# A graph-attention layer on one core: 39 output projections moved into the edge loop

## The reference

```
h     = relu(layernorm(x))
q,k,v = h wq + bq, h wk + bk, h wv + bv
score = q[dst].k[src] / 16 + edge_weight we + be        one number per edge
attn  = softmax of the scores of the edges with one destination
out   = sum over those edges of attn * v[src]
y     = layernorm(h + out + h ws + bs) g1 + b1
z     = layernorm(y + gelu(y w1 + b_ff1) w2 + b_ff2) g2 + b2
result = x + z
```

## Time and profile before

| | us |
|---|---|
| median of 3 runs (3053.38 to 3068.75) | 3056.34 |
| the profiled execution | 3050.0 |
| its span, first to last instruction | 3048.2 |
| PE busy, share of the span | 2431.4 (80%) |
| DVE | 1749.3 (57%) |
| POOL | 1632.3 (54%) |
| ACT | 1152.5 (38%) |

### The profile page before, as it was taken

One profiled execution on the slowest core, in us unless ns is written; L12 is line 12 of the kernel. 1 busy time (PEld: TensorE's weight loads), 2 busy tenths in 40 slices (PEclk: granted clock), 3 DMA queues, 4 the chain that ended last, 5 costly groups with the idle time before them and its releaser, 6 DMA issues. The chain is left out here.

```text
span 3048.2 us, 66637 instructions
## 1 busy us (share of the span) xinstructions
PE 2431.4 (80%) x15042; PEld 2006.5 (66%) x15043; DVE 1749.3 (57%) x7385; ACT 1152.5 (38%) x2601; POOL 1632.3 (54%) x1828
## 2 busy tenths in 40 slices
PE   6877778777777777787878778878877887879998
PEld 5666566666566666666666656666666666758897
DVE  7655555555455555555555555555555565557777
ACT  6433333333333333333333333333333333335666
POOL 5455555555555555555555555545555555451254
PEclk8988889888889889898888899999999898989999
DMA  7333333333333333333333333333333333233122
GB/s 237 97 106 108 108 108 102 108 96 113 95 104 104 104 97 106 102 105 104 97 100 97 102 93 102 108 90 99 102 101 106 92 101 105 86 98 103 52 82 66
DMA packets 148147, 311.29 MB, mean 102 GB/s; under 512 B 33566, under 2 KB 84625, under 8 KB 148104
## 3 DMA queue, kind: packets, MB, share of 16 engines
q0 software_dynamic: 75264, 205.62, 23.2%
q1 hardware_dynamic: 54718, 90.19, 9.1%
q10 hardware_dynamic: 18122, 14.96, 1.6%
HBM read 290.21 MB, written 20.43 MB: 102 GB/s over the span
## 5 line engine op out<-in xcount | busy, mean ns | idle before, releaser
L508 POOL DMA_INDIRECT work<-h_rows,idx x1536 | 1454.9, 947 | 1159.6 <-SPq L390 766.0
L1085 PE MATMUL bank<-work 128*128 x3528 | 1003.1, 410 | 125.7 <-ACT work L649 100.8
L1050 PE MATMUL bank<-q,onehot 128*128 x5316 | 746.0, 292 | 119.2 <-DVE norms L859 112.8
L1085 PEld LDWEIGHTS bank<-work 128*128 128x128 f32 x3528 | 652.9, 206 | 211.2 <-issue 143.8
L1050 PEld LDWEIGHTS bank<-q,onehot 128*128 128x128 bf16 x5316 | 548.6, 104 | 247.3 <-issue 99.5
L649 ACT COPY work<-bank 128x512 f32<-128x512 f32 x440 | 258.4, 587 | 1059.0 <-remote 609.9
L859 DVE SCALAR_TENSOR_TENSOR norms<-bank,work 128x257 bf16<-128x257 f32 x1326 | 503.8, 424 | 206.8 <-remote 167.4
L1056 PE MATMUL bank<-ident,mean 128*128 128x128 f32 x1764 | 296.7, 294 | 310.1 <-DVE mean L916 267.7
L1056 PEld LDWEIGHTS bank<-ident,mean 128*128 128x128 f32 x1764 | 211.0, 145 | 397.3 <-DVE mean L916 241.1
L859 DVE SCALAR_TENSOR_TENSOR work<-bank,work 128x257 bf16<-128x257 f32 x442 | 188.1, 425 | 445.1 <-remote 321.9
L916 DVE CUSTOM_DVE_ANT_0 work<-bank,work,mean 128x512 f32<-128x512 f32 x440 | 328.6, 747 | 115.7 <-issue 57.9
(11 more groups left out here) (200 smaller groups left out, 1726.9 us busy)
## 6 DMA issues: line engine op xcount, KB each, us to landing
dst_words<-dst_short SPq DMA_DIRECT2D x99, 512.0 KB
work<-h_rows,idx POOLq DMA_INDIRECT x1568
bias<-h_rows ACTq DMA_DIRECT2D x56, 128.0 KB
r_rows<-bias ACTq DMA_DIRECT2D x55, 128.0 KB
work<-r_rows SPq DMA_DIRECT2D x49, 128.0 KB, 2.6
h_rows<-acc SPq DMA_DIRECT2D x12, 512.0 KB, 6.8
work<-in_x SPq DMA_DIRECT2D x12, 512.0 KB, 3.9
out<-work SPq DMA_DIRECT2D x48, 128.0 KB, 1.8
```

Of the source, the lines that this page charges most:

```text
L508: pool.indirect_dma_start(rows[:, u, j, 0:D], None, h_rows, bass.IndirectOffsetOnAxis(idx[:, half, u * J + j:u * J + j + 1], 0)).then_inc( ...
L1050: last = nc.tensor.matmul(banks[j][:, 0:D1], onehot[:, k, j, :], q3[:, bass.ds(b, 1), c, 0:D1], start=(c == 0), stop=(c == 2))
L1085: last = nc.tensor.matmul(banks[6 + k][:, 0:D1], probs[k][:, j, :], rows[:, bass.ds(slot, 1), j, :], start=(j == 2), stop=(j == 1))
```

## The change

For blocks 0 to 38 (`LOOPED`) the trip computes all of y but its bias: `h (ws + 1) + bs + (sums / weight) wv`. The result is written over the block's sums in `acc`; nothing is stored in HBM. The other 10 blocks (`TAIL`) get both projections in the output stage.

- A block may be taken when its last step is done. ACT keeps the number of the next block in registers, and in step 2 of each trip reads the table of steps and moves on to the next block if that is ready, or else to a spare block (`NB`, zeros with a huge weight), whose result is thrown away (`choose_next`). The number of trips is the larger of what the steps need and 39 plus the largest lead, a lead being the trip in which a block is finished less its number.
- DVE floors and inverts all weights in step 0 of each trip. ACT weighs one block's sums in step 1.
- PE turns h at the end of steps 0 and 1, the weighed sums at the end of 2 and 3, and projects at the end of 5 and 6, each half with a bias matmul, two by ws and two by wv. wv is loaded once, before the loop, into rows that hold biases otherwise.
- ACT copies the turned halves in steps 1 to 4 before it copies the probabilities, and the halves of y in steps 6 and 7 behind the probabilities. L872 waits for these copies in the same steps.
- The store of r in the trip and the loads of r are gone. The output stage loads h of the 10 tail blocks, and PE turns both h and sums there. DVE adds weight * bv in place (one instruction where there were two) and takes the statistics; 30 looped blocks come among the tail's, 9 inside the feed-forward stage. The norm's factors are made for blocks 0 to 19, and later for the rest.

```diff
+    LOOPED = B * 4 // 5
+    TAIL = B - LOOPED
+    MOST_TRIPS = TRIPS + LOOPED + 1
+    ASIDE = 6
...
-        acc = sb("acc", [P, NB, D1])
+        acc = sb("acc", [P, NB + 1, D1])
...
-                def copy_r(turn, n):
-
-                    if n == 1:
-                        act.wait_ge(r_stored, turn * 16 + 16)
-                    act.wait_ge(r_ready, turn * 2 + (2 - n))
-                    nc.scalar.copy(r_out[:, n * P:(n + 1) * P], banks[6 + n][:, R_AT:R_AT + P]).then_inc(r_copied, 1)
-
-                def store_r(turn):
-
-                    act.wait_ge(r_copied, turn * 2 + 4)
-                    act.dma_start(r_rows[bass.ds(turn % B * P, P), :], r_out).then_inc(r_stored, 16)
+                def choose_next(r, i):
+
+                    at = table_place(act, place_in_table, i)
+                    act.load([last_seen], steps_tab[0:1, bass.ds(at + (U - 2), 1)])
+                    done = block_of(act, act.snap(last_seen, min_val=0, max_val=(B + 1) * CHUNKS) + r * ROUND)
+                    act.reg_alu(last_seen, act.to_reg(done), LOOPED, ALU.min)
+                    act.reg_add(block_next, next_block, 1)
+                    act.reg_alu(last_seen, last_seen, block_next, ALU.min)
+                    act.reg_sub(block_next, last_seen, block_next)
+                    act.reg_alu(block_next, block_next, 63, ALU.bitwise_and)
+                    act.reg_alu(block_next, block_next, next_block, ALU.bitwise_or)
+                    act.reg_alu(block_next, block_next, NB, ALU.min)
+                    act.reg_mov(next_block, last_seen)
+
+                def weigh_e(b):
+
+                    nc.scalar.activation(u_e, acc[:, bass.ds(b, 1), 0:D].rearrange("p a d -> p (a d)"), ACT.Copy, scale=inv_e[:, bass.ds(b, 1)]).then_inc(weighed, 1)
+
+                def copy_aside(turn, n, to, bank):
+
+                    act.wait_ge(side_ready, turn * ASIDE + n)
+                    nc.scalar.copy(to, banks[bank][:, R_AT:R_AT + P]).then_inc(side_copied, 1)
+
+                def copy_y(b, n):
+
+                    nc.scalar.copy(acc[:, bass.ds(b, 1), n * P:(n + 1) * P].rearrange("p a d -> p (a d)"), banks[6 + n][:, R_AT:R_AT + P]).then_inc(side_copied, 1)
...
-                        if steps == U and u in (2, 3):
-                            copy_hTe(act.snap(act.to_reg(r * NW + i), min_val=0, max_val=B * NW), u - 2)
-                        if steps == U and u in (5, 6):
-                            copy_r(act.snap(act.to_reg(r * NW + i), min_val=0, max_val=B * NW), 6 - u)
+                        if steps == U and u in (1, 2):
+                            copy_aside(turn, u, hT_e[:, (u - 1) * P:u * P], 6 + u % 2)
+                        if steps == U and u in (3, 4):
+                            copy_aside(turn, u, uT_e[:, (u - 3) * P:(u - 2) * P], 6 + u % 2)
+                        if steps == U and u == 1:
+                            act.wait_ge(inv_done, turn + 1)
+                        if steps == U and u in (6, 7):
+                            act.wait_ge(side_ready, turn * ASIDE + (u - 1))
                         act.wait_ge(turned, s + 1)
                         nc.scalar.copy(probs[k][:].rearrange("p j n -> p (j n)"), banks[5][:]).then_inc(probs_done, 1)
+                        if steps == U and u == 1:
+                            weigh_e(here)
+                        if steps == U and u in (6, 7):
+                            copy_y(here, u % 2)
+                        if steps == U and u == 2:
+                            choose_next(r, i)
+                            load_h_of_next()
...
+                        if steps == U and u == 0:
+                            turn = dve.snap(dve.to_reg(r * NW + i), min_val=0, max_val=B * NW)
+                            floor_at, aside = dve.to_reg(turn + 1), dve.snap(dve.to_reg(turn * ASIDE), min_val=0, max_val=B * NW * ASIDE)
+                            dve.wait_ge(added, step)
+                            nc.vector.tensor_scalar(floor_e, acc[:, 0:NB + 1, D], 1e-12, None, ALU.max).then_inc(floor_done, 1)
                         edge_scores(step_at(regs[u + 2]), r, prepared, k, meanwhile)
                         here = block_at(u)
+                        if steps == U and u == 0:
+                            dve.wait_ge(floor_done, floor_at)
+                            nc.vector.reciprocal(inv_e, floor_e).then_inc(inv_done, 1)
...
-                        if steps == U and u in (2, 3):
-                            dve.wait_ge(hTe_copied, dve.to_reg((r * NW + i) * 2 + (u - 1)))
-                        if steps == U and u in (5, 6):
-                            dve.wait_ge(r_copied, dve.to_reg((r * NW + i) * 2 + (u - 2)))
+                        if steps == U and u in (1, 2, 3, 4, 6, 7):
+                            dve.wait_ge(side_copied, dve.to_reg(aside + (ASIDE + u - u // 6)))
                         add_sums(s, u + 2, dve.snap(held[u], min_val=0, max_val=B) if u < 2 else blocks[u - 2])
...
+                def project_both(aside, n):
+
+                    y = banks[6 + n][:, R_AT:R_AT + P]
+                    if n == 0:
+                        pe.wait_ge(late_in, 5 * 16)
+                        pe.wait_ge(side_copied, aside + (ASIDE + 4))
+                    nc.tensor.matmul(y, onesb_rows, s_bias3[:, n * P:(n + 1) * P], start=True, stop=False)
                     for c in range(DC):
+                        nc.tensor.matmul(y, hT_e[:, c * P:(c + 1) * P], ws_sb[:, c, n * P:(n + 1) * P], start=False, stop=False)
+                    for c in range(DC):
+                        last = nc.tensor.matmul(y, uT_e[:, c * P:(c + 1) * P], wv_e[:, c, n * P:(n + 1) * P], start=False, stop=(c == DC - 1))
+                    last.then_inc(side_ready, 1)
...
-                        if steps == U and u in (1, 2):
-                            turn_h(pe.snap(pe.to_reg(r * NW + i), min_val=0, max_val=B * NW), u - 1)
-                        if steps == U and u in (4, 5):
-                            project_h(pe.snap(pe.to_reg(r * NW + i), min_val=0, max_val=B * NW), 5 - u)
+                        if steps == U and u in (0, 1):
+                            turn_h(turn, aside, u)
+                        if steps == U and u in (2, 3):
+                            turn_u(turn, aside, u - 2)
+                        if steps == U and u in (5, 6):
+                            project_both(aside, u - 5)
...
+                def add_bias(b):
+
+                    y = acc[:, b, 0:D]
+                    if b >= LOOPED:
+                        dve.wait_ge(o_ready, b - LOOPED + 1)
+                        y = banks[2 + tail_bank(b - LOOPED)][:, 0:D]
+                    nc.vector.scalar_tensor_tensor(out=acc[:, b, 0:D], in0=row_of["bv"], scalar=weight_sum[:, b:b + 1], in1=y, op0=ALU.mult, op1=ALU.add).then_inc(y_done, 1)
...
-                for b in range(3):
-                    add_bv(b)
-                add_output(0)
-                for b in range(1, B):
+                for n in range(AFTER_TAIL):
+                    b = y_order[n]
                     if b == B - 1:
                         copy_yT(0)
-                    add_output(b)
-                    measure(b - 1, y_done, FIRST_NORMS)
+                    next_y(n)
...
+                    for n in range(AFTER_TAIL + 2 * b, min(AFTER_TAIL + 2 * b + 2, B)):
+                        next_y(n)
```

More of the change, by code:

```diff
@@ L91, in gnn_layer @@
         wv_sb = sb("wv_sb", [P, DC, D])
[L92 to L95, removed]
+        bias = sb("bias", [P, 6, D])
+        row_of = {n: bias[:, k, :] for n, k in (("bs", 0), ("g1", 0), ("b2", 1), ("b_ff2", 2), ("bv", 3), ("g2", 4))}
+        h_in, hT_e, u_e = (bias[:, k, :] for k in range(3))
+        uT_e = u_e
+        wv_e = bias[:, 4:6, :]
         bff1_col = sb("bff1_col", [P, FC])
@@ L140, in gnn_layer @@
         ws_sb = wv_sb[:]
+        floor_e, inv_e = (ones[:, k * (NB + 1):(k + 1) * (NB + 1)] for k in range(2))
         wqk = halves(DC * D1)
@@ L1030, in _ @@
                         nc.tensor.matmul(chunk_of_step, shift_chunks, in_block, start=True, stop=True)
+                        nc.tensor.matmul(lead_row, lead_f, ident[:, 0:LOOPED], start=True, stop=True)
                         pe.wait_ge(falls_done, 2)
@@ L1114, in _ @@
                 keep_busy(banks[5], 14)
+                place_in_table = pe.alloc_register("place_in_table")
                 def trip(r, i, steps):
-                    pe.load(regs[0:steps + 3], steps_tab[0:1, bass.ds(i * U, steps + 3)])
+                    pe.load(regs[0:steps + 3], steps_tab[0:1, bass.ds(table_place(pe, place_in_table, i), steps + 3)])
+                    turn = pe.snap(pe.to_reg(r * NW + i), min_val=0, max_val=B * NW)
+                    aside = pe.snap(pe.to_reg(turn * ASIDE), min_val=0, max_val=B * NW * ASIDE)
                     first = pe.snap(pe.to_reg(r * TP + i * U), min_val=0, max_val=B * TP)
@@ L1171, in gnn_layer @@
         fT = slots(2, F)
+        both_T = fT
+        X_AT = used[0]
```

(39 more changed lines are left out.)

219 lines of the change are left out of this document (126 added, 93 removed).

## The result

The changed kernel takes 3206.05 us (median of 6 runs, 3188.02 to 3220.54) against 3058.07 us (6 runs, 3045.65 to 3068.84): 1.0477 times the time, 95% interval 1.0432 to 1.0522 (ratios here are of the runs' means). It is slower by 148 us; the forecast was 3138 in a range of 3030 to 3215.

The account below looks back on a forecast made before the run. It took a chain of hand-overs between engines, 6.07 us a step, to bound the edge stage. Edge +108 and output -26 gave +82 on the profiled 3050.0; 6 more for the median made 3138 us, range 3030 to 3215.

Parts of the forecast that it names:

- The loop that no longer stays loaded: Rival, edge stage: the longer trip fetches its code every trip, 114 us more, 3252 us; chance 0.04.
- Output stage, -26: Output stage: fewer DVE instructions per block bring the first feed-forward matmul 30 us after the first weighing, gaining 26 us.
- Copies of y, +44: Edge stage, steps 6 and 7: DVE's addition waits for ACT's copies behind the probabilities; 0.8 us a trip, 44 us.
- PE, +33: Edge stage: added turns and projection passes, 1.32 us a trip at full clock, partly hidden; 0.6 counted, 33 us.
- the 0.2 that was to show a larger share of PE: Sign: free steps near the edge stage's end growing over 0.2 us would mean PE's share was taken too small.
- ACT's code, +22: Edge stage, steps 1 and 2: weighing, table read, block choice and load of h cost 0.4 us a trip, 22 us.
- DVE, +14: Edge stage, step 0: floor and reciprocal of the weights cost 0.25 us a trip, 14 us.
- The -5 us for the store: Edge stage: dropping ACT's store of r at the trip's end saves 0.1 us a trip, 5 us.
- the rival that the holds swallow the added work: Rival, edge stage: gathers' end releases steps, so added work lies in existing waits; 3036 us, faster; chance 0.15.

Follow-up runs that it names:

- e2: The kernel before with 20 one-column memsets at VectorE's start, its loop otherwise untouched: 3119.75 us, ratio 1.0232 to the kernel before.
- e5: The changed kernel with 96 one-column memsets at VectorE's start, moving its loop: 3129.49 us, ratio 1.0126 to the kernel before.
- e12: e9 with ScalarE's weighing and block choice ahead of the probabilities' copy, 33 blocks in place of 40 before the feed-forward stage: 3094.09 us, ratio 0.9990.
- e9: Changed kernel, VectorE's loop moved on by 88; y copies ahead of the probabilities' copy, their wait on a one-column copy behind the mask's: 3106.45 us, ratio 1.0039.
- e6: e5 with the copies of y ahead of the probabilities' copy, waiting for the projection before the mask's copy: 3113.39 us, ratio 1.0062 to the kernel before.
- e8: e5 without the two wv passes in each of a trip's two projections: ratio 1.0115 to the kernel before.
- e10: e9 without ScalarE's block choice, PE's wv passes and VectorE's floor and reciprocal: 3085.14 us, ratio 0.9994 to the kernel before.
- e7: e5 without ScalarE's choice of the next block in step 2, always taking the spare one: ratio 1.0095 to the kernel before.
- e11: The kernel before with 96 memsets at VectorE's start: 3098.72 us, ratio 1.0018 to the kernel before.
- e1: The changed kernel with 40 one-column memsets at VectorE's start, nothing in the loop altered: 3206.1 us, ratio 1.0523 to the kernel before.
- e3: The changed kernel with ScalarE's copies of y ahead of the probabilities' copy, waiting for the projection before the mask's copy: 3165.55 us, ratio 1.0386.
- e4: The changed kernel with both e1's 40 memsets and e3's order of the copies of y: 3138.70 us, ratio 1.0292 to the kernel before.

## Why the prediction was right in direction and wrong in its sum

**The loop that no longer stays loaded** is the step that failed. The forecast read the earlier trace rows as a reason to leave it at 0.04: no trip fetches now. But 20 and 23 packets say only that the loop of today stays, not how near it is to its limit, and e2 shows that 20 instructions were enough. Its price, 114 us in the forecast, was measured at about 107 by e5, and at 71 to 122 by other pairs of runs. The loss is smaller than VectorE's 157 us of later first instructions (172 against 15 in e5), as steps 0 and 1 behind the stall shorten. That the time still fell inside the range is luck: a cost forecast at nothing was made up for in part by other terms that were forecast too high. The Trainium skill (Runtime: NRT & Kernel Launch, section Instruction fetch mechanics) has the rule that bears on it: a taken branch to a target outside the current two-page window waits for a fetch of that page. The five 8 KB packets in every trip agree with it in kind. It was cited, and then priced by a row that couldn't speak against it.

**Without it** the forecast was +82 us; e5's 1.0126 is +39 (20 to 57), so the other terms were forecast too high by some 40. Term by term:

- Output stage, -26: -22.3 from the last masking, -20.4 from the first weighing. The first feed-forward matmul comes 35.7 us after the first weighing, not 30 (the earlier trace rows had 56.1), as this timeline of the changed kernel shows:

```profile
2978.45 0.92 ACT L1343 ACTIVATE work<-acc,work 128x256 f32<-128x256 f32 x2 [5.39 <-DVE work L1440]
3008.97 0.60 ACT L1350 ACTIVATE work<-acc,norms 128x256 f32<-128x256 f32 x1 [9.00 <-DVE norms L271]
3009.62 0.69 PE L1564 MATMUL bank<-ident,work 128*128 128x128 f32 x2 [5.12 <-ACT work L1350]
3010.35 1.91 PE L1556 MATMUL bank<-wv_sb,work 128*128 128x256 f32 x4
3014.13 0.61 PE L1582 MATMUL bank<-work,dst_words 128*128 128x128 f32 x4
```

  DVE's 40 blocks and their norms' factors took some 30 us (from 2978.45 to just before 3008.97), as forecast. What was missed is what follows them: ScalarE's first normalising waits for the norm's factors, which DVE works out last, PE waits 5.12 us for ScalarE, and four passes behind that wait take 1.91 us (see the last section). PE waited 1.5 us for the loads of h. e12, with seven blocks fewer ahead, ends the stage 30.3 us after its first weighing.

- Copies of y, +44: 27 us (e5 to e9, 0.0087; 7 to 46 by the intervals). The mechanism was right, DVE waiting for L656 in steps 6 and 7; by the maskings the time was lost in step 6 for the most part. The two runs are of different chips, and e6 against e5 on one chip gives 20 us for another order. A third of e5's wait remains in e9, so some of the 44 may still be there.

- PE, +33: e8 took out the passes with wv, two thirds of PE's added work, and moved the ratio by 0.0011, inside its interval. PE's busy time in a trip rose from 38.0 to 39.6 us (1959 and 1907.53 of 2500, times 48.45 and 51.90), about the 1.5 forecast, and hardly any of it shows in the time. The free steps near the end answer to the earlier trace rows; the first four rows enclose three steps with a turn, the next step has no work aside, and the last one has a projection:

```profile
2944.31 0.60 PE L1118 MATMUL bank<-ident,mean 128*128 128x128 f32 x4
2948.37 0.60 PE L1118 MATMUL bank<-ident,mean 128*128 128x128 f32 x4
2952.43 0.60 PE L1118 MATMUL bank<-ident,mean 128*128 128x128 f32 x4
...
2956.48 0.60 PE L1118 MATMUL bank<-ident,mean 128*128 128x128 f32 x4
...
2960.43 0.60 PE L1118 MATMUL bank<-ident,mean 128*128 128x128 f32 x4
...
2965.37 0.60 PE L1118 MATMUL bank<-ident,mean 128*128 128x128 f32 x4
```

  A free step with a turn takes 4.06 us, one without work aside 3.95 (2956.48 to 2960.43), one with a projection 4.94. In the kernel before the last was 4.50, from these rows:

```profile
2778.48 0.60 PE L1056 MATMUL bank<-ident,mean 128*128 128x128 f32 x4
...
2782.98 0.60 PE L1056 MATMUL bank<-ident,mean 128*128 128x128 f32 x4
```

  So a projection added the 0.44 us that was forecast, and a turn 0.11, half of the 0.22 that was read from the weight loads of the earlier trace rows: 1.10 us a trip in free steps in place of 1.32. Over a trip of free steps that is 0.14 us a step, below the 0.2 that was to show a larger share of PE.

- ACT's code, +22, DVE, +14: with PE's passes 14 us together (e10), not 56 with PE's full share of them. ScalarE's wait for its own issue ahead of the exponentials, 68.1 us before, was to grow by 1 to 2 us a trip. In the changed kernel, where DVE's maskings come late, it fell to 26.5 us; in e5, without them, it grew by 47 us in some 46 trips:

```profile
ACT mean L669 <- issue: 115.4, 73, 3.6
```

  The size was right, and yet the time hardly moves when the code is gone (e7).

- What is left: e10's ratio of 0.9994 with 22 us gained in the output stage leaves about 20 us in the edge stage for the weighing, two more copies and two more turns, less what the store gave. That is a subtraction and was not tested by itself; in the two profiled executions of e10 and e11, on one chip, the first and the last masking stand 2704.9 and 2705.8 us apart, so the rest may be nothing. The -5 us for the store were not tested either.

So the rival that the holds swallow the added work was half true: of the 56 us forecast for what e10 takes out 14 are measured, but DVE's wait for a copy that stands behind the held one is not swallowed.

## What to carry to other kernels

Before adding instructions to a loop, ask how far its code is from the limit at which it is loaded again: the packets of the instruction queues per trip tell on which side it is, not how near; a run with a few dummy instructions ahead of the loop tells both, and once found the cure may be as cheap as a shift. Work added to PE, ScalarE and VectorE in this loop, where engines often wait for a late hand-over, cost little; a copy queued behind such a hand-over, with another engine waiting for it, cost some 27 us that a change of its place gave back.

## What the runs showed of the hardware

VectorE's loop of 320 or 325 instructions was loaded again in each trip, by 5 packets of 8 KB, when it lay in four pieces some 126 recorded instructions long (the changed kernel, e1, e2, e3, e4), and never when it lay in three (the kernel before, e5, e11 and the others). The borders of the pieces are worked out from where the packets start. A refetch held the engine 3.2 us (0.28 without), and up to 5.0. Why it takes five packets for four pieces is open.

TensorE's clock fell in the output stage, after idle time. In the changed kernel PE stood 5.12 us without work. Its granted clock, 1.00 (2.4 GHz) from 3002.0 to 3004.5 us, was 0.50 (1.2 GHz) from 3009.6 to 3014.0, and four passes took 1.91 us (the row at 3010.35). e12 had idled 1.94 us at the same place. There the clock was 1.00 from 2892.0 to 2893.4 us and 0.53 from 2893.4 to 2895.5: the first four passes took 1.03 us, and the next four 1.87:

```profile
2891.95 0.44 PE L1568 MATMUL bank<-ident,work 128*128 128x128 f32 x2 [1.94 <-ACT work L1354]
2892.62 1.03 PE L1560 MATMUL bank<-wv_sb,work 128*128 128x256 f32 x4
2893.49 1.87 PE L1562 MATMUL bank<-bias,work 128*128 128x256 f32 x4
```
